# Self- and cross-attention pairs of a decoder: two program orders laid over each other, unit by unit

## The chip, the core and the metric

The kernel runs on one core of one Trainium2 chip. The metric is the device time of one execution in microseconds; the figure of a kernel is the median of its runs. One more execution was recorded by the hardware profiler, and the views shown below are of that execution. The engines are called by their short names: PE (TensorE), PEld (its weight loads), DVE (VectorE), ACT (ScalarE), POOL (GpSimd), SP (SyncE, which here issues nearly all DMAs).

## The reference

A decoder of twelve sub-layers with x of shape (4, 256, 128), each sub-layer `x = x + f(layernorm(x))`. Two stretches of it matter here, the pairs self-attention then cross-attention of layer 0 (sub-layers 0 and 1) and of layer 3 (sub-layers 9 and 10). Shortened:

```python
def attention(q, k, v, mask):             # 16 heads of width 8, B = 4 batches, 256 queries
    s = q @ k.T * 8 ** -0.5 + mask        # 256 keys (self) or 512 keys of the context (cross)
    return softmax(s) @ v                 # the softmax takes each row's maximum off
x = x + attention(heads(norm(x) @ Wq + bq), heads(norm(x) @ Wk + bk), ...) @ Wo + bo   # self
x = x + attention(heads(norm(x) @ Wq + bq), heads(ctx @ Wk + bk), ...) @ Wo + bo       # cross
```

The cross-attention's queries come from the x that the self-attention of the pair has made. Its keys and values come from the context, which is there from the start. Layer 0's cross-attention has a mask of one row for each batch, and layer 3's two attentions have full masks.

## The kernel before

An attention works in 16 steps (G = 16), one for each batch (4) and group of four heads (4). A step s has these parts, in a software pipeline: `a` are the scores for the maxima (PE, banks 0 to 3 of PSUM), reduced by DVE; `split` turns the maxima into three bf16 parts (POOL); `turn` transposes them (PE, bank 7), ACT copies them out, SP writes them into the rows of `qs` as further rows of the queries; `b` are the scores the other way round, with the maxima now taken off (PE, banks 4 and 5), and ACT's exponent; `av` multiplies by the values (PE, bank 6), `o` copies that out (ACT), `o_tp` transposes it (PE, bank 7) and DVE divides; after every fourth step `oT` and `y` transpose and multiply by the output weights (PE, bank 7) and DVE adds the result to x.

`order()` (L1118) yields these parts one after the other, and every engine walks through the same order and issues its own piece of each part. So the order on every queue is written by hand here, and a semaphore wait at the head of a queue holds everything behind it. `order_plain` (L1178) serves layer 0, `order_masked` (L1124) layer 3. The plain order runs over steps and, inside a step, units: four for the self-attention, eight for the cross-attention. The masked order runs over units alone, two to a step for self and four for cross. In both the last `a` part is followed by a tail in which only `b`, `av`, `o_tp`, `oT` and `y` of the last steps are left: units 68 to 91 of layer 0's self-attention, units 33 to 44 of layer 3's.

The two attentions of a pair know each other as `next` and `prev`. Keys of the cross-attention are made before the self-attention starts and split and spilled to DRAM beside it. The norm of x, and from it the cross-attention's queries, goes batch by batch: `stats_vector`, `h_vector`, `hT_tensor` and `q_tensor` (the names `n_stats`, `n_h`, `n_tp`, `nq` in the order) for batches 0 and 1 run inside the self-attention, those for batches 2 and 3 inside the cross-attention. The values (`val`, `v_sb`: four matmuls of 128x128 and a bias addition, for each of four chunks) are made in the cross-attention's first steps. `ahead_at` and `ahead_masked_at` (L511, L526) say at which step and unit; `ahead_sync` (L486) does the same for SP.

PE starts the cross-attention after it has waited for `x_done` of the self-attention, which DVE sets after the last addition to x (L2868, L2899). PE then waits in `stack_landed` (L764) for `first_quad`: the DMAs that bring the keys and queries of batch 0 and, for layer 0, the mask rows of all four batches.

The instructions of the rows below: L794 `a` scores, L872 and L860 their reductions (plain, and cross masked), L908 `turn`, L939 and L840 `b` scores, L803 masks added on PE, L1025 `av`, L1114 the addition to x, L563 values, L442 a subtraction of the query's parts, L264 POOL's addition of the output bias to x, L453 and L484 SP's spill and load of the cross queries.

## Time and profile before

| | us |
|---|---|
| median of 3 runs | 1468.37 |
| lowest, highest run | 1465.16, 1477.7 |
| span of the profiled execution | 1486.9 |
| its busy time on PE, DVE, ACT, POOL | 1203.9, 898.9, 707.4, 273.3 |
| mean granted clock of PE in it | 0.885 of full |

The profiled execution has no other time of its own than its span; that is 18.5 us, or 1.3%, above the median of the runs. The page cuts the span in 40 slices of 37.2 us. The first pair's self-attention lies in slices 1 to 3 and its cross-attention from there on (it starts at 110.8 us); the second pair's cross-attention starts at 1312.9 us, in slice 36. The granted clock is 1.00 at 2.4 GHz and 0.50 at 1.2 GHz; a value between them is a mean over both.

### The profile page before, as it was taken

The page shows a single profiled execution, that of the slowest core. Times are in us where ns is not written, and L with a number is a line of the kernel's source. Part 1 is how long each engine was busy: PE and PEld are TensorE (multiplying, and loading weights), DVE is VectorE, ACT ScalarE, POOL GpSimd, SP SyncE. Part 2 cuts the span into 40 slices and gives each one's busy share as a digit, 9 for nine tenths or more (in the row PEclk, how much of TensorE's full clock was granted, in tenths as well). Part 3 has the DMA queues.
Part 4 walks back from the last instruction along what each step waited for, and adds up shares of the span by engine and source line. Part 5 has one row for each costly group of instructions (what it writes and reads, how often), then busy time and mean ns, then how long its engine had stood idle before and what let it go on. Part 6 is the DMA issues. An engine that isn't in the chain of part 4 may idle for free. (4 is left out here: it accounts for less than half of the span.)

```text
span 1486.9 us, 26591 instructions
## 1 busy us (share of the span) xinstructions
PE 1203.9 (81%) x9482; PEld 745.1 (50%) x9489; DVE 898.9 (60%) x2315; ACT 707.4 (48%) x1440; POOL 273.3 (18%) x549
## 2 busy tenths in 40 slices
PE   4878997785786487567999999999957768979983
PEld 2333434683343487355666666666636733333331
DVE  5758865335667344775676676666741076667746
ACT  3654881221632121213665665666713425636663
POOL 3412111452010254100000000000006504211110
PEclk9897998897797699777999999999988878979996
DMA  7321242793401585000000000000046543211100
GB/s 189 89 57 44 67 140 100 230 290 116 115 30 64 169 252 181 28 1 1 1 1 1 1 1 1 1 1 1 1 112 193 169 131 82 54 42 50 48 6 15
DMA packets 87892, 114.34 MB, mean 77 GB/s; under 512 B 10945, under 2 KB 67982, under 8 KB 87294
## 3 DMA queue, kind: packets, MB, share of 16 engines
q1 hardware_dynamic: 83314, 103.52, 23.5%
q0 software_dynamic: 4448, 9.12, 2.0%
q8 instruction: 78, 1.28, 0.4%
q14 instruction: 52, 0.43, 0.1%
HBM read 85.79 MB, written 25.82 MB: 75 GB/s over the span
## 5 line engine op out<-in xcount | busy, mean ns | idle before, releaser
L1025 PE MATMUL ps<-probs,vaug 128*32 128x256 f32 (+1 forms) x1792 | 145.7, 399 | 15.3 <-ACT probs L991 8.5
L2508 DVE CUSTOM_DVE_ANT_0 wring<-ps,probs 128x768 f32<-128x768 f32 x128 | 122.6, 958 | 57.3 <-PE ps L2380 56.8
L2464 ACT COPY qs<-ps 128x768 f32<-128x768 f32 x128 | 102.3, 800 | 97.7 <-PE ps L2387 97.7
L982 ACT ACTIVATE probs<-ps 128x512 f32<-128x512 f32 x192 | 104.2, 595 | 63.7 <-PE ps L840 63.5
L872 DVE TENSOR_REDUCE mx<-ps 128x2 f32<-128x1024 f32 (+1 forms) x96 | 114.7, 1220 | 21.0 <-PE ps L794 20.7
L986 ACT ACTIVATE probs<-ps 128x512 f32<-128x512 f32 x192 | 106.4, 595 | 39.6 <-PE ps L939 37.6
L244 POOL TENSOR_TENSOR rstd<-veps,mhalf 128x8 f32<-128x8 f32 x12 | 19.9, 1660 | 569.5 <-DVE veps L229 539.9
L2446 ACT ACTIVATE wring<-wring,r 128x768 f32<-128x768 f32 x128 | 120.8, 944 | 2.9 <-DVE r L2511 2.9
L2387 PE MATMUL ps<-ident,wring 128*128 128x128 f32 x768 | 110.3, 281 | 3.2 <-DVE wring L2545 3.2
L2387 PEld LDWEIGHTS ps<-ident,wring 128*128 128x128 f32 x768 | 84.5, 141 | 39.4 <-issue 35.3
L1808 POOL DMA_INDIRECT scr_y<-probs x85 | 82.9, 975 | 99.4 <-DVE probs L1765 82.5
L2380 PE MATMUL ps<-probs 64*128 64x512 f32 (+1 forms) x512 | 99.9, 508 | 1.1 <-DVE r L2508 1.0
L860 DVE CUSTOM_DVE_ANT_0 wring<-ps,m3x 128x512 f32<-128x512 f32 x128 | 83.3, 689 | 26.1 <-PE ps L794 15.6
L794 PE MATMUL ps<-ks,qs 49*128 49x256 bf16 (+1 forms) x512 | 82.1, 362 | 12.5 <-DVE mx L872 3.5
L1557 PE MATMUL ps<-probs,wring 128*128 128x128 f32 x428 | 84.0, 304 | 8.9 <-DMA wring<-in_L_ffn_w 4.7
L2395 PE MATMUL ps<-qs,ks 128*64 128x256 f32 x768 | 89.9, 383 | 1.0 <-ACT qs L2464 1.0
L1758 DVE TENSOR_TENSOR probs<-gated,ps 128x256 f32<-128x256 f32 (+1 forms) x62 | 32.1, 519 | 88.1 <-ACT gated L1614 49.7
L2545 DVE TENSOR_SCALAR wring<-wring,r 128x768 f32<-128x768 f32 x128 | 79.5, 621 | 4.5
L1570 PE MATMUL ps<-wring,probs 128*128 128x128 f32 x428 | 64.1, 289 | 18.1 <-DVE probs L1758 8.5
L1557 PEld LDWEIGHTS ps<-probs,wring 128*128 128x128 f32 x428 | 67.9, 213 | 14.1 <-DMA wring<-in_L_ffn_w 7.5
L1614 ACT ACTIVATE gated<-ps 128x256 f32<-128x256 f32 (+1 forms) x62 | 28.6, 463 | 95.6 <-PE ps L1559 71.7
L1025 PEld LDWEIGHTS ps<-probs,vaug 128*32 128x32 f32 x1792 | 37.4, 110 | 65.8 <-issue 61.7
(346 smaller groups left out, 2387.0 us busy)
## 6 DMA issues: line engine op xcount, KB each, us to landing
wring<-in_L_ffn_w SPq DMA_DIRECT2D x19, 768.0 KB
wring<-in_L_ffn_w SPq DMA_DIRECT2D x32, 384.0 KB
wring<-in_L_ffn_w SPq DMA_DIRECT2D x19, 514.0 KB
qs<-scr_q SPq DMA_DIRECT2D x18, 192.0 KB
qs<-scr_qx SPq DMA_DIRECT2D x16, 192.0 KB
probs<-in_L_ffn_w SPq DMA_DIRECT2D x8, 384.0 KB
probs<-in_L_ffn_w SPq DMA_DIRECT2D x4, 768.0 KB
scr_k<-probs SPq DMA_DIRECT2D x21, 128.0 KB, 2.8
```

Source lines behind the costliest of these rows:

```text
L860: dve.tensor_tensor_reduce(wring[:, k % 2, r * S2:(r + 1) * S2], bank(self.banks(0, k)[r]), m3x[:, 0, a % 2 * S2:(a % 2 + 1) * S2], 1.0, - ...
L872: dve.tensor_reduce(out, src, AX.X, ALU.max, negate=True).then_inc(a_max.sem, 1)
L982: act.activation(probs[:, s % 2, 2 * c + r, kt0 * S:(kt0 + 2) * S], bank(self.banks(3, k)[r]), ACT.Exp).then_inc(p_exp.sem, 1)
L986: act.activation(probs[:, s % 2, 2 * c + r, kt0 * S:(kt0 + 2) * S], bank(4 + k % 2), ACT.Exp).then_inc(p_exp.sem, 1)
L1025: ins = pe.matmul(ps[32 * j:32 * j + 32, self.av_bank(s), q0:S], vaug[:, s % 2, kt, j, :], probs[:, s % 2, j, at:at + S - q0], start=(kt = ...
L1557: ins = pe.matmul(bank(k % 2)[:, at], gate[:, at], cols, start=True, stop=True)
L2380: ins = pe.matmul(bank(2 * j + lo // 512, 0, hi - lo), self.qT[rows, g % 2, k * P:(k + 1) * P], self.kT[rows, g % 3, lo:hi], start=True, s ...
L2387: ins = pe.transpose(self.buffer("turn", i, t * P, t * P + P), self.sc[:, i % 4, t * P:(t + 1) * P], ident[:, :])
L2395: ins = pe.matmul(self.buffer("sum", i, 0, S)[HW * j:HW * j + HW, :], self.v[:, i % 3, t, j * HW:(j + 1) * HW], self.pT[:, i % 2, j, t, :] ...
L2446: act.activation(self.sc[:, i % 4, :], self.sc[:, i % 4, :], ACT.Exp, bias=self.neg[:, i % 4:i % 4 + 1], accum_out=self.tot[:, i % 4:i % 4 ...
L2464: act.copy(self.pT[:, g % 2, j, :, k * P:(k + 1) * P], self.buffer("turn", i, 0, KV).rearrange("p (t n) -> p t n", n=P)).then_inc(self.out ...
L2508: dve.tensor_tensor_reduce(self.sc[:, s, :], src, self.maskb[:, u // (2 * PR), :], 1.0, -3.0e38, ALU.add, ALU.max, self.top[:, s:s + 1]).t ...
```

## The change

The separate orders are cut into functions of one unit (`plain_steps`, `causal_steps`, `masked_steps`), and `order()` of the self-attention now walks through both attentions of the pair. Up to the unit behind the self-attention's last `turn` it yields only the self-attention's parts. From there on each turn of the loop yields the self-attention's next unit and then the cross-attention's next unit, until the self-attention has none left. The cross-attention's own program and PE's wait for `x_done` are gone.

```diff
         def order(self):
-            return self.order_masked() if self.mask == "full" else ...
+            then = self.next
+            handoff = (33 if self.mask == "full" else 17 * self.u) if then else self.units()
+            for i in range(max(self.units(), handoff + then.units() if then else 0)):
+                if i < self.units():
+                    for step in self.steps(i):
+                        yield self, *step
+                if i >= handoff:
+                    for step in then.steps(i - handoff):
+                        yield then, *step
...
+        def partner_tensor(self, pe):
+            t = self.prev or self.next
+            if not t:
+                return
+            for sem, count in ((m_sb, t.turns), (o_div, t.outs), (oT_sb, t.turned_outs), (y_out, t.ys)):
+                if count and self.seen.get(sem.sem.name) != count:
+                    pe.wait_ge(sem.sem, sem.at(t.n, count))
+                    self.seen[sem.sem.name] = count
...
-            if s not in (0, 7, 11):
+            fused = s in subs and subs[s].prev
+            if s not in (0, 7, 11) and not fused:
                 pe.wait_ge(x_done.sem, x_done.at(s - 1, 1))
...
-    first_quad = counter("first_quad", [8 + 8 * int(c["mask"] == "row") if c["cross"] else 4 ...
+    first_quad = counter("first_quad", [8 + 2 * int(c["mask"] == "row") if c["cross"] else 4 ...
+    row_in = new("row_in")
...
+                if self.mask == "row" and s == NQ:
+                    pe.wait_ge(row_in, 32 * (B - 1))
...
-            if 12 <= g < 15:
-                self.q_spill_sync(sp, 0, g - 12)
-            if g == 15:
+            for k in ((0,), (1, 2))[g - 12] if g in (12, 13) else ():
+                self.q_spill_sync(sp, 0, k)
+            if g == 14:
                 self.q_load_sync(sp, 0)
...
-            if self.next and 7 <= o < 13 and o % 4 in (3, 0):
+            if self.next and o >= 7 and o % 4 in (3, 0):
                 yield ("n_tp" if o % 4 else "nq"), (o - 7) // 4, o
...
-                steps = {(0, 1): [("n_tp", 2), ("hT", 2)], (0, 3): [("nq", 2), ("qf", 2), ("n_h", 3)], (0, 6): [("val", 0)], (1, 0): [("val", 1)],
-                         (1, 1): [("v_sb", 0)], (1, 2): [("val", 2)], (1, 3): [("qr", 2), ("qp2", 2)], (1, 4): [("v_sb", 1)], (1, 5): [("v_sb", 2)],
-                         (2, 0): [("val", 3)], (2, 1): [("v_sb", 3), ("qp3", 2)], ...
+                steps = {(1, 0): [("val", 0)], (1, 2): [("val", 1), ("v_sb", 0)], (1, 4): [("nq", 2), ("qf", 2), ("v_sb", 1)],
+                         (1, 6): [("qr", 2), ("qp2", 2)], (1, 7): [("val", 2)], (2, 0): [("v_sb", 2), ("qp3", 2)], (2, 1): [("val", 3)],
+                         (2, 3): [("v_sb", 3)], (2, 4): [("n_h", 3)], ...
...
-                    if self.prev and s == 1:
-                        bias_gpsimd(pool, self.sub, self.norm, f"{self.name}_o")
+                if self.prev and s == 3:
+                    bias_gpsimd(pool, self.sub, self.norm, f"{self.name}_o")
```

Besides, PE gets waits that the barrier made needless before: the cross-attention's first use of each PSUM bank (in `a_tensor`, `b_tensor`, `masked_tensor`, `av_tensor`, `value_tensor`, `q_tensor`) waits for the self-attention's last reader of that bank, and `partner_tensor` does so for bank 7, which `turn`, `o_tp`, `oT` and `y` of both attentions share. POOL's addition of the output bias to x moves from the cross-attention's step 1 to step 3. `ahead_masked_at` moves the values by one or two units in the same way as `ahead_at`.

PE at the first hand-over. Before, from the self-attention's `oT` of batch 2 on (L939 is `b`, L1025 `av`, L1059 `o_tp`, L1104 `y`); the first `a` of the cross-attention stands seven rows below the last one shown:

```order
L1082 MATMUL ps<-ident,o 128x128 x2
L939 MATMUL ps<-qs,ks 128x256 x2
L1025 MATMUL ps<-probs,vaug 32x256 x4
L1059 MATMUL ps<-ident,osb 128x128 x2
L939 MATMUL ps<-qs,ks 128x256 x2
L1104 MATMUL ps<-w,oT 128x128 x2
L939 MATMUL ps<-qs,ks 128x256 x2
L1025 MATMUL ps<-probs,vaug 32x256 x4
L939 MATMUL ps<-qs,ks 128x256 x4
L1025 MATMUL ps<-probs,vaug 32x256 x4
L1059 MATMUL ps<-ident,osb 128x128 x2
L939 MATMUL ps<-qs,ks 128x256 x4
```

After, from the same place (L970 is `b`, L1058 `av`, L1093 `o_tp`, L1140 `y`, and L808 with `ks,qs 128x512` is `a` of the cross-attention):

```order
L1117 MATMUL ps<-ident,o 128x128 x2
L808 MATMUL ps<-ks,qs 128x512 x2
L970 MATMUL ps<-qs,ks 128x256 x2
L1058 MATMUL ps<-probs,vaug 32x256 x4
L1093 MATMUL ps<-ident,osb 128x128 x2
L970 MATMUL ps<-qs,ks 128x256 x2
L1140 MATMUL ps<-w,oT 128x128 x2
L808 MATMUL ps<-ks,qs 128x512 x2
L970 MATMUL ps<-qs,ks 128x256 x2
L1058 MATMUL ps<-probs,vaug 32x256 x4
L970 MATMUL ps<-qs,ks 128x256 x2
L808 MATMUL ps<-ks,qs 128x512 x2
```

The first `a` scores of the cross-attention, 18 rows behind this `oT` before, now stand right behind it and ahead of seven of the self-attention's last eight `b` parts; one more `a` follows every two units.

SP's queue at the same place. Before, from the maxima of step 13 on (`qs<-mT`; `scr_qx<-` are spills of the query's parts, `ks<-mrow` mask rows, `qs<-scr_qx` the load of batch 0's queries):

```order
L742 DMA qs<-mT 3x2x256 x2
L460 DMA ks<-mrow 1x8x512 x2
L453 DMA scr_qx<-lg 128x2x256
L742 DMA qs<-mT 3x2x256 x2
L460 DMA ks<-mrow 1x8x512 x2
L453 DMA scr_qx<-r 128x256
L742 DMA qs<-mT 3x2x256 x2
L484 DMA qs<-scr_qx 48x8x256 x2
```

After:

```order
L752 DMA qs<-mT 3x2x256 x2
L464 DMA ks<-mrow 1x8x512 x2
L457 DMA scr_qx<-lg 128x2x256
L457 DMA scr_qx<-r 128x256
L752 DMA qs<-mT 3x2x256 x2
L464 DMA ks<-mrow 1x8x512 x2
L489 DMA qs<-scr_qx 48x8x256 x2
L752 DMA qs<-mT 3x2x256 x2
```

The third spill and the load of the queries have moved ahead of one pair of `qs<-mT` each.

DVE at the second hand-over. Before, from the division of step 13 on (L1068 and L1069 are a division, L860 is the reduction of the cross-attention, in two rows):

```order
L1068 RECIPROCAL rsum<-ps 128x8
L1069 TENSOR_TENSOR o<-ps,rsum 128x2x32
L1068 RECIPROCAL rsum<-ps 128x8
L1069 TENSOR_TENSOR o<-ps,rsum 128x2x32
L1114 TENSOR_TENSOR x<-x,ps 128x256
L373 BN_STATS stats<-x 128x6 x2
L376 BN_AGGR mv<-stats 128x2 x2
L378 TENSOR_SCALAR veps<-mv 128x2
L2868 ISA
L860 ISA wring,mx<-ps,m3x 128x512
L860 ISA mx 128x1
L860 ISA wring,mx<-ps,m3x 128x512
```

After, from the self-attention's statistics of batch 2 on (L878 is the reduction, L390 the norm of batch 2, L1102 and L1103 a division):

```order
L380 TENSOR_SCALAR veps<-mv 128x2
L878 ISA wring,mx<-ps,m3x 128x512
L878 ISA mx 128x1
L878 ISA wring,mx<-ps,m3x 128x512
L878 ISA mx 128x1
L390 TENSOR_SCALAR h<-x,mv,rstd 128x128 x2
L878 ISA wring,mx<-ps,m3x 128x512
L878 ISA mx 128x1
L878 ISA wring,mx<-ps,m3x 128x512
L878 ISA mx 128x1
L1102 RECIPROCAL rsum<-ps 128x8
L1103 TENSOR_TENSOR o<-ps,rsum 128x2x32
```

Before, all of the self-attention's divisions and its last statistics stood ahead of the first reduction. Now two units of reductions (four instructions of L878 with a read each) stand ahead of the division of step 13.

## Rows read from the trace of the kernel before

**Rows 1.** Windows of the first pair; columns as its first line says.
```profile
core 0: us, PE busy (x) PEld busy (x) DVE busy (x) ACT busy (x) POOL busy (x), PEclk, DMA share, GB/s
93.78:139.10 45.32, 36.54 (x224) 15.48 (x226) 29.43 (x48) 18.71 (x41) 7.28 (x19) 0.70 0.16 41
...
97.30:104.00 6.70, 6.50 (x40) 2.24 (x40) 2.75 (x12) 3.80 (x8) 0.98 (x2) 0.51 0.49 117
104.00:111.00 7.00, 3.40 (x32) 1.56 (x28) 2.19 (x10) 1.21 (x4) 0.15 (x1) 0.98 0.01 2
111.00:119.00 8.00, 8.00 (x34) 4.71 (x33) 7.03 (x9) 1.25 (x3) 1.35 (x5) 0.57 0.01 3
119.00:126.00 7.00, 4.63 (x33) 2.75 (x33) 6.94 (x9) 2.11 (x5) 1.48 (x5) 0.91 0.21 58
126.00:138.50 12.50, 10.93 (x68) 3.16 (x66) 9.11 (x8) 6.90 (x14) 3.13 (x7) 0.51 0.12 32
150.00:200.00 50.00, 49.51 (x514) 20.64 (x516) 43.81 (x53) 43.62 (x87) 8.70 (x40) 1.00 0.22 58
```

**Rows 2.** The same view of the second pair.
```profile
1298.75:1343.21 44.46, 34.05 (x235) 14.96 (x233) 26.98 (x87) 15.56 (x35) 7.75 (x21) 0.73 0.15 37
1306.00:1313.00 7.00, 3.23 (x28) 1.54 (x28) 2.19 (x10) 1.36 (x4) 0.00 (x0) 0.97 0.04 11
1313.00:1322.60 9.60, 8.47 (x30) 4.81 (x30) 6.97 (x22) 1.25 (x3) 1.75 (x6) 0.50 0.01 2
1322.60:1329.60 7.00, 4.04 (x31) 2.22 (x31) 6.45 (x19) 1.75 (x4) 0.76 (x4) 0.99 0.21 57
1329.60:1343.00 13.40, 11.54 (x76) 3.85 (x76) 7.79 (x25) 5.20 (x12) 4.31 (x10) 0.50 0.12 32
1350.00:1430.00 80.00, 75.42 (x881) 28.07 (x873) 64.98 (x209) 56.82 (x120) 14.62 (x66) 1.00 0.16 40
```

**Rows 3.** Timeline of the first hand-over: start, us, engine, line, operation, idle before.
```profile
92.90 0.44 SPq L453 DMA_DIRECT2D scr_qx<-r  x1
...
93.78 0.38 PE L939 MATMUL ps<-qs,ks 52*128 52x256 bf16 x2
...
94.80 0.39 PE L939 MATMUL ps<-qs,ks 52*128 52x256 bf16 x2
...
95.96 0.93 SPq L484 DMA_DIRECT2D qs<-scr_qx  x2
...
110.79 0.39 PE L794 MATMUL ps<-ks,qs 49*128 49x512 bf16 x2 [1.54 <-DVEq L2868]
```

**Rows 4.** The second pair's first cross scores, the same view.
```profile
1312.94 0.61 PE L794 MATMUL ps<-ks,qs 49*128 49x512 bf16 x2 [1.54 <-DVEq L2868]
```

**Rows 5.** Timeline: `av` at half and full clock, a subtraction between them.
```profile
99.16 1.08 PE L1025 MATMUL ps<-probs,vaug 128*32 128x256 f32 x8
...
100.07 0.43 DVE L442 TENSOR_TENSOR gated<-gated 128x256 bf16<-128x256 f32 x1
...
104.57 0.64 PE L1025 MATMUL ps<-probs,vaug 128*32 128x256 f32 x8 [0.54 <-ACT osb L1042]
```

**Rows 6.** Bias addition, the subtraction beside it, and cross step 4's first scores.
```profile
125.32 2.35 POOL L264 TENSOR_TENSOR x<-x,brow 128x1024 f32<-128x1024 f32 x1
125.70 2.25 DVE L442 TENSOR_TENSOR r<-comb,lg 128x256 bf16<-128x256 f32 x1
...
139.10 0.39 PE L794 MATMUL ps<-ks,qs 49*128 49x512 bf16 x2
```

**Rows 7.** The second hand-over: third spill of the queries, and the unit behind 1298.75.
```profile
1295.60 0.42 SPq L453 DMA_DIRECT2D scr_qx<-r  x1
...
1301.33 0.40 PE L803 MATMUL ps<-m3a,identb 64*64 64x512 bf16 x2
```

**Rows 8.** DMA issues around the first hand-over: count, KB each, us to landing.
```profile
scr_qx<-gated SPq DMA_DIRECT2D x1, 192.0 KB, 3.4
```

**Rows 9.** The page, costliest groups: the plain reduction (count, busy, mean ns, idle before).
```profile
L872 DVE TENSOR_REDUCE mx<-ps 128x2 f32<-128x1024 f32 (+1 forms) x96 | 114.7, 1220 | 21.0 <-PE ps L794 20.7
```

More of the change, by code:

```diff
@@ L548, in evicted @@
         def evicted(self, o):
-            if self.next and 7 <= o < 13 and o % 4 in (3, 0):
+            if self.next and o >= 7 and o % 4 in (3, 0):
                 yield ("hT" if o % 4 else "qf"), (o - 7) // 4, o
@@ L1115, in y_vector, with units @@
                               ALU.add).then_inc(y_out.sem, 1)
-        def order(self):
-            return self.order_masked() if self.mask == "full" else self.order_causal() if self.mask == "causal" else self.order_plain()
-        def order_masked(self):
+        def units(self):
+            if self.mask == "full":
+                return G * self.u + self.behind + 4 * self.u
+            if self.mask == "causal":
+                return 2 * (G + 6)
+            return (G + self.lag + 4) * self.u
@@ new lines, in steps @@
+        def steps(self, i):
+            if self.mask == "full":
+                return self.masked_steps(i)
+            return (self.causal_steps if self.mask == "causal" else self.plain_steps)(*divmod(i, 2 if self.mask == "causal" else self.u))
+        def order(self):
+            then = self.next
[7 more added lines that the diff above has]
+                        yield then, *step
@@ L1178, in order_plain @@
-        def order_plain(self):
+            v = t - self.behind - n
+            o, d = v // n, v // n - 1
+            if t < G * n + self.behind:
+                yield "masked", t, 0
+            if v % n == 0 and 0 <= o < G:
+                yield from self.beside(o)
+            if self.cross:
+                if 0 <= o < G:
+                    yield "av", o, v % n
+                if v % n == 0 and last(d - 1):
+                    yield "y", (d - 1) // NQ, 0
+                if t % n == 1 and 0 <= t // n - 1 < G:
+                    yield "turn", t // n - 1, 0
+                if v % n == 2 and 0 <= d < G:
+                    yield "o_tp", d, 0
+                if v % n == 3 and last(d):
+                    yield "oT", d // NQ, 0
+            else:
+                if v % n == 1 and last(d):
+                    yield "oT", d // NQ, 0
+                if v % n == 0 and last(d - 1):
+                    yield "y", (d - 1) // NQ, 0
+                if 0 <= o < G:
+                    yield "av", o, v % n
+                if t % n == 0 and 0 <= t // n - 1 < G:
+                    yield "turn", t // n - 1, 0
+                if v % n == 0 and 0 <= d < G:
+                    yield "o_tp", d, 0
@@ new lines, in vector, with vector_step @@
+        def vector(self, dve):
+            for who, what, s, u in self.order():
+                who.vector_step(dve, what, s, u)
+        def vector_step(self, dve, what, s, u):
+            if what == "a":
+                self.a_vector(dve, s, u)
+            elif what == "masked" and s < G * self.u:
+                self.a_vector(dve, *divmod(s, self.u))
+            elif what == "b" and not self.maximum:
+                self.clip_vector(dve, s, u)
+            elif what == "o_tp":
+                self.div_vector(dve, s)
+            elif what == "y":
+                if self.n == 1 and s == B - 1:
+                    masks_vector(dve)
+                self.y_vector(dve, s)
+            elif what == "v_sb":
+                self.value_vector(dve, s)
+            elif what == "n_stats":
+                (self.next or self).stats_vector(dve, s)
+            elif what == "n_h":
+                (self.next or self).h_vector(dve, s)
+            elif what == "qr":
+                (self.next or self).q_r_vector(dve, s)
+            elif what == "qp3":
+                (self.next or self).q_p3_vector(dve, s)
@@ new lines, in scalar, with scalar_step @@
+        def scalar(self, act):
+            for who, what, s, u in self.order():
+                who.scalar_step(act, what, s, u)
+        def scalar_step(self, act, what, s, u):
+            if what == "b":
+                self.b_scalar(act, s, u)
+            elif what == "masked" and s >= self.behind:
+                self.b_scalar(act, *divmod(s - self.behind, self.u))
+            elif what == "o":
+                self.o_scalar(act, s)
+            elif what == "oT":
+                self.oT_scalar(act, s)
+            elif what == "turn":
+                self.turn_scalar(act, s)
+                if self.next and s < B:
+                    self.next.key_p2_scalar(act, s)
+            elif what == "hT":
+                if u >= 0:
+                    act.wait_ge(av_mm.sem, av_mm.at(self.n, u + 1))
+                (self.next or self).hT_scalar(act, s)
+            elif what == "qf":
+                if u >= 0:
+                    act.wait_ge(av_mm.sem, av_mm.at(self.n, u + 1))
+                (self.next or self).q_scalar(act, s)
+            elif what == "qp2":
+                (self.next or self).q_p2_scalar(act, s)
```

289 lines of the change are left out of this document (121 added, 168 removed).

## The prediction

> **What bounds the kernel now.** The table of busy times has PE at 1203.9 of 1486.9 us, far ahead of DVE, so work of other engines beside a busy PE is mostly hidden. I cut each pair into windows. In the middle of the first pair's cross-attention PE is busy 49.51 of 50 us and DVE 43.81, at full clock; in the second pair's PE is busy 75.42 of 80 us and DVE 64.98 [rows 1, 2]. That is what a well filled stretch looks like, and there is nothing to gain there. Around the hand-overs it differs. From 93.78 us, when the self-attention has made its last turn of maxima, to 139.10 us, when the cross-attention's step 4 begins, 45.32 us pass, with PE busy 36.54 us at a mean clock of 0.70 and DVE 29.43 [rows 1]. The second pair has the like from 1298.75 to 1343.21 us: 44.46 us, PE 34.05 at 0.73, DVE 26.98 [rows 2]. I then asked what PE waits for. The timeline puts the idle time before the first cross scores at 110.79 and at 1312.94 us down to DVEq L2868, the barrier after the last addition to x [rows 3, 4]. Before each barrier there are 7 us in which PE is busy only 3.40 and 3.23 us, because the tail of the self-attention is a chain of round trips; behind it, in the first cross steps, DVE is the busy one (7.03 of 8.00 us) [rows 1, 2]. So two stretches with complementary needs lie one behind the other.
>
> The windows show a second cost. After each thin stretch PE's granted clock is near 0.5, that is 1.2 GHz: at 97.3 to 104, 111 to 119 and 126 to 138.5 us in the first pair, at 1313 to 1322.6 and 1329.6 to 1343 us in the second [rows 1, 2]. The same `av` group takes 1.08 us there and 0.64 us at full clock [rows 5], a factor of 0.6. Of PE's 36.54 us, 25.43 lie in the three half-clock windows (6.50 + 8.00 + 10.93); at full clock they would be 15.3, so PE's work in the first stretch is 26.4 us. In the second, 20.01 us lie in such windows (8.47 + 11.54) and become 12.0, which makes 26.0 us.
>
> **The change part by part.** *Removed:* the wait for `x_done`, and with it the serial order of tail and start. *Added:* nothing that computes. Every matmul, reduction and DMA is issued as before, so only their overlap counts. *The sum for the first pair*, to the same point (cross step 4's first scores, [rows 6]): DVE needs 29.4 us. Of this 1.8 us is one subtraction (L442) that took 2.25 us beside POOL's bias addition of 2.35 us [rows 6] and would take 0.43 as elsewhere [rows 5], since the bias addition now runs two steps later, where DVE has reductions only. That leaves 27.6. A filled stretch takes 50 / 43.81 = 1.14 times its DVE work [rows 1], hence 31.5. DVE can't begin at once: I add 2.0 us until its first cross reduction (below), and 2.0 us for the first half-clock spell. This one I expect to stay, because what comes before it (up to 97.3 us) is not merged; PE's 6.5 us of it hold only 3.9 of work, a loss of 2.6 of which DVE's slack covers a part. Together 35.5 us against 45.3, **9.8 us less**. Bounds of this term: if PE and DVE overlapped without loss, the longer of the two would be about 30 (PE 26.4 + 2.6 + the stall of 1.4; DVE 27.6 + 2.0), 15 us less; with nothing overlapped, 0.
>
> *The second pair:* DVE 27.0 us times 80 / 64.98 = 1.23 is 33.2, and 1.5 us until the first reduction gives 34.7 against 44.5, **9.8 us less**. PE's 26.0 us fit with room. I take no half-clock spell here, since the clock is still 0.97 from 1306 to 1313 us, at the end of the tail [rows 2].
>
> *The load of the queries.* PE's first cross scores wait for it, and the self-attention's `b` parts are queued behind them, then ACT's exponents and `av`. In the second pair the third spill left at 1295.60 us, behind the maxima of step 14 [rows 7], and the load followed the maxima of step 15; now both move up by one, the load to about 1295.6. With 3.4 us to landing, the time of a spill of the same 192 KB [rows 8], it is there at 1299, before PE is through the unit whose successor began at 1301.33 [rows 7]. Hidden. In the first pair the load moves from 95.96 to about 93.1 us: it takes the place of the spill at 92.90, a few tenths later because the spill now stands ahead of the maxima [rows 3]. PE reaches the new scores at about 94.8, where the next `b` stood [rows 3]. The load lands between 96.2, if it is as fast as 3.1 us, and 97, at 3.4 us behind its second half's issue: a stall of 1.4 to 2.2 us; I take 1.4 because nothing else is on the queues then. It is inside the 2.0 us above.
>
> *The moved values, queries and mask rows.* All are the same instructions, inside the sum. The mask rows of batches 1 to 3 no longer hold the start; only the two for batch 0 do, and those are old by then. The row of batch 1 waits for the self-attention's last `b`, and the maxima of cross step 0 are queued behind it on SP. That `b` comes near 106 us by my order, the maxima at about 113: hidden, and worth at most 1.4 us (one pair of issues) if not.
>
> *The added waits.* DVE's divisions and additions to x, four and two in each tail, now stand behind cross reductions, and PE's `o_tp`, `y` and `turn` wait for them. The wait costs nothing while PE has cross work queued ahead of it, and a reduction, 1.2 us [rows 9], each where it has not. The factors 1.14 and 1.23 come from stretches with just this coupling.
>
> The sum is 9.8 + 9.8 = 19.6 us. What follows each pair starts from its end and moves up whole. The profiled span of 1486.9 would be 1467.3; against the median of 1468.4, 18.5 us lower, the same 19.6 us give **1449 us**.
>
> Of the subtraction: the Trainium skill, SBUF — State Buffer, "Who interferes with whom", says a DVE instruction with two SBUF inputs is held while GpSimd reads SBUF, and one with at most one is not. By that rule the trace's 2.25 us [rows 6] is such a hold and the reductions, which read PSUM, run freely beside the bias addition. Were they held too, the 1.8 us would stay where they are and the time would be 1451.
>
> **The rivals.** *The clock stays low.* PE and DVE now wait for each other in short turns all through the merged stretch, and the clock might fall again there as it did at 126 and 1329.6 us. For it: those falls came after 7 us with PE busy 4.63 and 4.04 [rows 1, 2], and the merged stretch isn't far from that. Against it: a merged stretch has PE busy 26.4 of 35 us or more, 75%, and in the filled stretch the same coupling holds 1.00. Price: a spell of 12.5 us, as at 126, in each pair loses 0.4 x 12.5 = 5 us each: 1459 us. The skill's TensorE: Matmul & The Clock Gate, "A second HAM failure mode: psum-queue depth-cycling", tells of a clock that swings because of just such small pauses; the windows of the filled stretches show none.
>
> *Nothing overlaps.* Each unit's self part and cross part wait for one another, so that the merged units take as long as both did: 1467 us. Against it speaks that the first `a` and `b` parts use different banks and no data of each other. For it, that all queues keep their order.
>
> *Slower.* The place is the six waits of PE for DVE in each tail (four divisions, two additions). If each is exposed for a reduction of 1.2 us or two, and nothing overlaps besides, 12 x 1.2 to 1.5 = 16 us come on top: 1484. It decides once exposed waits exceed the overlap, some 1.6 us for each of the 12.
>
> *More than forecast.* PE and DVE overlap without loss: 15 + 14 us, 1439.
>
> **How the numbers follow.** The forecast with its own range 1441 to 1456 has 0.62, the low clock 0.20, nothing overlapped 0.10, slower 0.04, more than forecast 0.04. The range 1440 to 1463 leaves out nothing overlapped, slower and part of the last, some 0.18. A measurement of this kernel tells about 1% from no change, that is 14.7 us: faster means under 1453.7. The forecast gives that in nine of ten cases (0.57), more than forecast 0.04, a low clock in one of the pairs only 0.04: 0.65. Slower is 0.04, and the rest 0.31.
>
> **What would show it.** The same two stretches, from the first `b` after the last turn to cross step 4 in the first pair and to unit 14 in the second, take 35.5 and 34.7 us. The wait for DVEq before the first cross scores is gone. PE waits 1.4 us for the load of the queries near 94.8. The clock is low once after 97 us and not again in the pair, and near 1.00 in the second pair. DVE is over 80% busy between the hand-over and step 4. The 2.25 us subtraction takes 0.43. The prediction is wrong if the clock falls again inside the merged stretch, if DVE is under 75% busy there with PE idle before `o_tp` or `y`, or if a wait for `first_quad` exceeds 3 us.

## The result, and the profile after

| | before | after |
|---|---|---|
| median, us | 1470.97 (4 runs, 1465.16 to 1477.7) | 1450.86 (4 runs, 1449.63 to 1456.17) |
| ratio after to before | | 0.9873, 95% interval 0.9838 to 0.9907 |
| span of the profiled execution | 1486.9 | 1447.8 |
| mean granted clock of PE in it | 0.885 | 0.894 |

The changed kernel is 1.27% faster by the ratio of the runs, some 18.7 us on 1471; the medians are 20.1 us apart. The two profiled spans differ by 39.1 us, but not all of that is the change. From the fourth cross turn of pair 1 to turn 15 of pair 2 the program is the same in both kernels (but for the end of POOL's bias addition in its first microsecond), and this part took 1156.04 us before (142.51 to 1298.55) and 1137.89 after (134.02 to 1271.91). A second execution of the changed kernel, in an experiment below, took 1153.57 us for it. So some 18 us of the 39 are differences between executions. I read the two stretches of the prediction alone.

Line numbers move: L808 is `a`, L890 and L878 its reductions (plain, masked), L937 `turn`, L970 `b`, L817 masks on PE, L571 values, L660 their bias addition on DVE, L446 the query's subtraction, L265 the output bias on POOL, L464 mask rows, L489 the load of the cross queries, L752 the maxima into `qs`. In a window's row the number behind x counts the instructions, and the value third from the end is the mean granted clock.

Windows of the changed kernel, pair 1, from the first `b` after the self-attention's last turn (91.70 us) to cross step 4's first scores (130.76); this answers to [rows 1]:

```profile
core 0: us, PE busy (x) PEld busy (x) DVE busy (x) ACT busy (x) POOL busy (x), PEclk, DMA share, GB/s
91.70:130.76 39.06, 31.35 (x224) 14.10 (x224) 27.49 (x48) 18.31 (x42) 4.83 (x18) 0.78 0.16 44
95.90:105.30 9.40, 9.28 (x51) 3.51 (x53) 6.32 (x16) 3.54 (x7) 0.93 (x2) 0.50 0.09 24
105.30:111.00 5.70, 5.64 (x56) 3.28 (x51) 4.46 (x7) 1.35 (x3) 0.80 (x4) 0.99 0.02 3
...
114.00:117.00 3.00, 1.41 (x13) 0.67 (x11) 3.00 (x5) 1.66 (x4) 0.83 (x4) 1.00 0.38 108
...
120.00:122.50 2.50, 1.19 (x10) 0.37 (x8) 2.50 (x3) 2.07 (x6) 0.58 (x2) 0.99 0.00 1
122.50:129.50 7.00, 6.60 (x46) 2.11 (x48) 5.62 (x7) 3.70 (x8) 1.49 (x6) 0.52 0.20 57
```

The stretch took 39.06 us, where 45.32 were before and 35.5 were forecast: 6.3 us less instead of 9.8. The clock is at 0.50 for 9.4 us right from the first cross scores, and again at 0.52 for 7 us from 122.5 on. Ahead of this second fall PE is busy 1.41 of 3 us (114 to 117) and 1.19 of 2.5 us (120 to 122.5) while DVE is busy all the time; between the two PE is well filled, 2.83 of 3 us.

The same view of pair 2, from 1272.11 us to the turn at 1304.39; it answers to [rows 2]:

```profile
1272.11:1304.39 32.28, 27.45 (x234) 12.86 (x233) 25.64 (x85) 14.83 (x34) 5.38 (x20) 0.89 0.15 39
1275.00:1290.00 15.00, 13.47 (x122) 6.84 (x120) 13.83 (x50) 6.13 (x15) 1.98 (x7) 1.00 0.17 46
...
1292.50:1304.39 11.89, 9.85 (x74) 4.34 (x75) 8.79 (x26) 4.92 (x10) 2.32 (x8) 0.71 0.14 36
1293.00:1297.00 4.00, 3.94 (x22) 2.39 (x24) 3.29 (x11) 1.32 (x3) 0.20 (x1) 0.57 0.00 1
1297.00:1300.00 3.00, 1.53 (x20) 0.57 (x16) 2.79 (x8) 2.01 (x4) 0.29 (x1) 1.00 0.46 116
1300.00:1304.39 4.39, 4.39 (x38) 1.38 (x35) 2.21 (x7) 1.59 (x4) 1.34 (x6) 0.61 0.06 17
```

Here 32.28 us stand against 44.46 before and 34.7 forecast: 12.2 us less. From 1275 to 1290 us both engines are full, PE 90% and DVE 92% busy at full clock. Only behind that, from 1292.5 on, the mean is 0.71: two short low spells of the clock, with 1.00 between them.

Timeline of the first hand-over (SPq is SP's DMA queue; behind "x" the idle time before and its releaser), answering to [rows 3]:

```profile
91.01 0.65 SPq L464 DMA_DIRECT2D ks<-mrow  x1
...
91.70 0.38 PE L970 MATMUL ps<-qs,ks 52*128 52x256 bf16 x2
91.70 0.95 SPq L489 DMA_DIRECT2D qs<-scr_qx  x2
...
95.90 0.61 PE L808 MATMUL ps<-ks,qs 49*128 49x512 bf16 x2 [3.12 <-DMA qs<-scr_qx]
...
96.62 1.23 DVE L890 TENSOR_REDUCE mx<-ps 128x2 f32<-128x1024 f32 x1 [3.09 <-PE ps L808]
```

The wait for DVEq is gone, and PE now reaches the cross scores at 92.78 (95.90 less 3.12) and waits 3.12 us for the load of the queries. The load was issued from 91.70 on, behind a mask row, and released PE 4.2 us later. In three more profiled executions of this pair's program (they belong to the experiments below) the wait was 2.94, 3.70 and 3.85 us. DVE's first cross reduction starts at 96.62, 4.9 us into the stretch.

Timeline of the second hand-over, which answers to [rows 4, 7]:

```profile
1268.96 0.93 SPq L489 DMA_DIRECT2D qs<-scr_qx  x2
...
1274.69 0.39 PE L808 MATMUL ps<-ks,qs 49*128 49x512 bf16 x2
```

The load leaves 5.7 us ahead of the scores, and PE doesn't wait. Timeline of DVE, POOL and PE near 117 and 132 us, answering to [rows 6]:

```profile
116.78 0.41 DVE L446 TENSOR_TENSOR r<-comb,lg 128x256 bf16<-128x256 f32 x1
...
116.92 1.16 PE L571 MATMUL ps<-w,ctxT 128*128 128x128 f32 x8 [1.32 <-DVE v L660]
...
132.42 2.37 POOL L265 TENSOR_TENSOR x<-x,brow 128x1024 f32<-128x1024 f32 x1
133.46 2.43 DVE L890 TENSOR_REDUCE mx<-ps 128x2 f32<-128x1024 f32 x2 [0.96 <-PE ps L808]
```

The subtraction takes 0.41 us where it took 2.25. The bias addition now runs beside two reductions, which take 2.43 us together, as long as elsewhere (1.22 and 1.23 each).

### The profile page after: what moved, and what is told of

It reads as the page before. It is cut to its first block, busy times and chain, and to the rows that moved or that the text cites. A ratio compares the mean times of both kernels' runs of the same rounds, so it can differ in the third digit from the quotient of the medians.

```text
span 1447.8 us, 26607 instructions
## 1 busy us (share of the span) xinstructions
PE 1185.1 (82%) x9482; PEld 735.6 (51%) x9489; DVE 896.5 (62%) x2315; ACT 708.3 (49%) x1440; POOL 273.0 (19%) x549
## 4 chain that ended last, share of the span: by engine, by line
PE 62%; DVE 14%; DMA 6%; ACT 6%; issue 5%; POOL 4%; SPq 3%; DVEq 0%; another core or an unknown queue 0%; ACTq 0%; POOLq 0%
PE ps L2447 7%; PE ps L2454 6%; PE ps L1058 6%; PE ps L2462 6%; PE ps L808 4%; PE ps L2434 3%; PE ps L817 3%; PE ps L1624 2%; PE ps L970 2%; PE ps L2428 2%; DMA wring<-in_L_ffn_w 2%; PE ps L1637 2%; PE ps L2961 2%; PE ps L1626 2%; PE ps L1093 2%
## 5 line engine op out<-in xcount | busy, mean ns | idle before, releaser
L1058 PE MATMUL ps<-probs,vaug 128*32 128x256 f32 (+1 forms) x1792 | 145.2, 398 | 12.1 <-ACT probs L1022 7.1
L890 DVE TENSOR_REDUCE mx<-ps 128x2 f32<-128x1024 f32 (+1 forms) x96 | 115.0, 1221 | 21.3 <-PE ps L808 20.7
L878 DVE CUSTOM_DVE_ANT_0 wring<-ps,m3x 128x512 f32<-128x512 f32 x128 | 83.2, 688 | 20.0 <-PE ps L808 11.7
L808 PE MATMUL ps<-ks,qs 49*128 49x256 bf16 (+1 forms) x512 | 80.6, 354 | 9.9 <-DMA qs<-scr_qx 3.1
L1624 PE MATMUL ps<-probs,wring 128*128 128x128 f32 x428 | 80.3, 294 | 7.9 <-DMA wring<-in_L_ffn_w 5.6
L1058 PEld LDWEIGHTS ps<-probs,vaug 128*32 128x32 f32 x1792 | 37.3, 110 | 61.3 <-issue 56.6
L2447 PEld LDWEIGHTS ps<-probs 64*128 64x128 f32 x512 | 44.3, 186 | 47.0 <-issue 38.0
```

The source lines that it names most:

```text
L808: ins = pe.matmul(bank(at[r], i * self.keys, (i + 1) * self.keys), self.qv(s, c, r, ROWS_A, t * P, (t + 1) * P), self.kv(s, c, r, ROWS_A), ...
L890: dve.tensor_reduce(out, src, AX.X, ALU.max, negate=True).then_inc(a_max.sem, 1)
L1058: ins = pe.matmul(ps[32 * j:32 * j + 32, self.av_bank(s), q0:S], vaug[:, s % 2, kt, j, :], probs[:, s % 2, j, at:at + S - q0], start=(kt = ...
L1624: ins = pe.matmul(bank(k % 2)[:, at], gate[:, at], cols, start=True, stop=True)
L2447: ins = pe.matmul(bank(2 * j + lo // 512, 0, hi - lo), self.qT[rows, g % 2, k * P:(k + 1) * P], self.kT[rows, g % 3, lo:hi], start=True, s ...
```

## The experiments

All stretches below run from turn 15 (the self-attention's last) to the cross-attention's fourth turn, since these marks are in every kernel. The work in them is nearly the same everywhere: 29.2 to 29.9 us of DVE in pair 1 (31.7 before), 30.8 to 31.6 in pair 2. Each median stands beside that of the kernel before on the same chip; there the kernel before takes 1486.82 to 1487.58 us, not 1470.97. The last two columns are one profiled execution's stretches, in us, and the mean clock in them:

| kernel | median, us | ratio to before (95%) | pair 1 | pair 2 |
|---|---|---|---|---|
| before | 1470.97 | 1 | 49.11 at 0.72 | 51.75 at 0.77 |
| changed | 1450.86 | 0.9873 (0.9838, 0.9907) | 42.71 at 0.80 | 39.64 at 0.91 |
| serial | 1482.84 | 0.9965 (0.9938, 0.9991) | 47.78 at 0.75 | 45.72 at 0.89 |
| first pair only | 1473.79 | 0.9904 (0.9867, 0.9942) | 41.96 at 0.80 | 47.64 at 0.82 |
| second pair only | 1473.64 | 0.9926 (0.989, 0.9962) | 45.74 at 0.85 | 38.64 at 0.96 |
| masks behind | 1469.20 | 0.9878 (0.9843, 0.9912) | 41.52 at 0.79 | 41.98 at 0.84 |
| changed, again | 1466.81 | 0.9892 (0.9844, 0.9939) | 43.03 at 0.80 | 38.55 at 0.96 |
| filled | 1464.60 | 0.9847 (0.9806, 0.9889) | 40.67 at 0.87 | 39.63 at 0.91 |
| masks behind and filled | 1466.22 | 0.9872 (0.9826, 0.9919) | 37.04 at 0.95 | 38.63 at 0.96 |
| one step later | 1467.51 | 0.9898 (0.9854, 0.9941) | 39.05 at 0.91 | 38.61 at 0.96 |
| changed, third | 1468.69 | 0.9887 (0.9854, 0.992) | 43.12 at 0.80 | 40.05 at 0.91 |
| masks behind and filled, again | 1466.90 | 0.9886 (0.9851, 0.9921) | 36.28 at 0.95 | 38.63 at 0.96 |
| one step later, again | 1468.81 | 0.9885 (0.9851, 0.9919) | 43.20 at 0.72 | 38.62 at 0.96 |
| serial, bias at step 1 | 1485.39 | 0.9992 (0.9964, 1.0019) | 51.91 at 0.67 | 49.40 at 0.79 |

The pair 2 column shows how much one execution may differ from the next: ten rows have the changed kernel's program there. Six of them took 38.55 to 38.64 us at 0.96, three 39.63 to 40.05 at 0.91, and one 41.98 at 0.84. So a difference of up to 3 us between two single stretches proves nothing by itself.

**Serial: everything of the change but the merge.**

```diff
-            handoff = (33 if self.mask == "full" else 17 * self.u) if then else self.units()
+            handoff = self.units()
```

> The changed kernel with the hand-over put back to the end of the self-attention in both pairs: its new order functions, added waits, earlier query load and later values stay, only the overlap is gone. If the overlap is the whole of the gain (the prediction's sum), this is the kernel before within 0 to 3 us less, because PE no longer waits for the barrier's semaphore (1.54 us idle in each pair before): ratio to before 0.998 to 1.000. If the new placement of the values and of the query load brings part of it by itself, the ratio is near 0.995 or below. If the added waits cost something that the overlap hides, it is above 1.002.

The rest of the change (values one or two units later, bias at step 3, the queues' new order, no `x_done`) brings 0.35% by itself, 4.0 us between the medians. The merge is what is left, about 0.8% (0.9873 to 0.9892 for the changed kernel against 0.9965). Windows of the serial kernel's two stretches:

```profile
93.01:140.79 47.78, 38.15 (x260) 16.53 (x256) 29.68 (x50) 21.56 (x48) 7.39 (x23) 0.75 0.18 46
1298.21:1343.93 45.72, 35.00 (x310) 15.90 (x311) 31.58 (x101) 20.12 (x45) 7.92 (x26) 0.89 0.14 40
```

In pair 2 this is 6.0 us less than before at the same DVE work (31.62 before), and PE's busy time falls from 41.01 to 35.00 us for 311 and 310 matmuls in the record: the mean clock is 0.89 instead of 0.77. After PE's first thin spot in the cross steps the clock fell before (1329.6 us on, [rows 2]) and did not here. That the moved values did this isn't shown: it is one execution of each kernel.

**One pair alone.** The first-pair-only kernel has `self.units()` in place of 33, the second-pair-only kernel in place of `17 * self.u`.

> Only the first pair (layer 0) is merged, the second pair runs one attention after the other. The prediction's sum gives 9.8 us for this pair: ratio 0.9933. The trace of the changed kernel, read over the same stretch, gives 45.3 - 39.1 = 6.3 us: ratio 0.9957. The rival that the pairs share the gain evenly and one profile is off would show 0.9935 here and in the other half.

> Only the second pair (layer 3) is merged. The prediction's sum gives 9.8 us: ratio 0.9933. The trace of the changed kernel gives 44.5 - 32.3 = 12.2 us: ratio 0.9917. If the parts add up, the two halves' gains together are the 18.7 us of the whole change.

```profile
92.64:134.60 41.96, 34.15 (x260) 15.38 (x256) 29.59 (x50) 21.06 (x48) 7.27 (x23) 0.80 0.20 52
```

```profile
1293.45:1332.09 38.64, 33.03 (x310) 14.52 (x311) 30.79 (x101) 19.97 (x45) 7.97 (x26) 0.96 0.17 47
```

The first row is of the first-pair-only kernel, the second of the other. Against the serial kernel pair 1 gains 5.8 us in its stretch and pair 2 7.1 us; by the medians each merge is worth 9.1 and 9.2 us, each with an uncertainty of some 6 us. Neither merge needs the other: each merged stretch is as short alone as in the changed kernel. That the medians add up holds only within these uncertainties (18.3 us for the two alone, some 0.8% or 12 us for both). The pair that is not merged has the serial kernel's program once more, and is as long as there within 2.1 us, both ways: 45.74 us at 0.85 in pair 1 and 47.64 at 0.82 in pair 2. Against the kernel before, the rest of the change thus brings 4.1 or 6.0 us in pair 2 by the execution taken.

**Masks behind: the queries' load ahead of the last mask rows on SP.**

```diff
-            if self.mask == "row" and g in (10, 13, 14):
-                self.mask_sync(sp, (0, 2, 3)[(10, 13, 14).index(g)])
+            if self.mask == "row" and g == 10:
+                self.mask_sync(sp, 0)
...
+            if self.mask == "row" and g in (13, 14):
+                self.mask_sync(sp, g - 11)
```

> The changed kernel with one edit on SP's queue: the mask rows of batches 2 and 3 are issued behind the third spill and behind the load of batch 0's queries instead of ahead of them (1.4 us of issue each). In the changed kernel PE is idle for 3.12 us before its first cross scores, for this load. Theory that the load is late because of what SP issues ahead of it: the load leaves 1.4 us earlier, the idle time falls to about 1.7 us, and the time by 1 to 1.5 us against the changed kernel (ratio to before about 0.9865). Rival, that the landing of the two halves of 192 KB sets it or that the clock's low spell swallows it: the idle time stays over 2.5 us or the time doesn't move.

```profile
90.75 0.93 SPq L489 DMA_DIRECT2D qs<-scr_qx  x2
91.72 1.43 SPq L464 DMA_DIRECT2D ks<-mrow  x2
...
94.66 0.61 PE L810 MATMUL ps<-ks,qs 49*128 49x512 bf16 x2 [1.73 <-DMA qs<-scr_qx]
```

The wait falls from 3.12 to 1.73 us, 1.4 us, which is one pair of mask issues (1.43), and the stretch by 1.2 us (by 0.4 against the first-pair-only kernel, whose pair 1 is the changed one's). So the mask rows ahead of the load are some 1.4 us of the stall; the prediction had left them where they were. The clock did not gain by it: it was low behind the shorter wait too, 0.79 over the stretch. The ratio is that of the changed kernel within its interval.

**Filled: does PE's pause cost the clock?**

```diff
+            if k == 0 and n == 1:
+                pe.wait_ge(a_max.sem, a_max.at(0, a_max.totals[0] - 1))
+                for _ in range(2):
+                    pe.matmul(bank(0), wt(f"{self.name}_q"), ctxT[:, 0:512], start=True, stop=True, ...)
             if a == 0:
                 self.stack_landed(pe, s)
```

> The changed kernel once more, beside the next three on one chip. Both theories: 1.2 to 1.3% faster than the kernel before (ratio 0.987), with PE waiting about 3 us for the queries' load before the cross-attention's first scores in pair 1, and low clock from there for some 9 us and again near 122 us.

> Two more matmuls, 128x512 in f32 out of data that is there, are put on PE ahead of its wait for the first quad of the cross-attention in pair 1; their result is overwritten. They fill about 1.7 of the 3.1 us that PE waits there. Theory A (the pause makes the clock fall, and the low clock stretches PE's work behind it): the granted clock stays at 1.00 from 96 to 104 us, the stretch from turn 15 to the fourth cross turn shrinks from 42.7 by 1 to 3 us, and the kernel runs 1 to 2.5 us faster than the changed one. Theory B (the clock costs little there, since DVE's reductions are the bound of these units): the clock may rise but the stretch stays at 42.7 within 0.7 us, and so does the time.

> Masks of batches 2 and 3 behind the queries' load on SP's queue, as in the run with the masks behind, which left PE a wait of 1.73 us, and one more 128x512 matmul (0.85 us) in this wait. Theory A (clock): 1.00 from 95 to 104 us, 2.5 to 4 us faster than the changed kernel over both edits. Theory B (no gain from the clock): as the masks alone, 1.2 us less in the stretch than the changed kernel.

The changed kernel repeats itself closely, 43.03 us at 0.80, with a wait of 3.70 us for the load. In the filled kernel 1.86 us of the wait remain and the stretch is 2.4 us shorter. In the third, whose wait is filled but for 0.67 us, it is 6.0 us shorter. The first cross scores of the three, in this order:

```profile
98.50 0.61 PE L808 MATMUL ps<-ks,qs 49*128 49x512 bf16 x2 [3.70 <-DMA qs<-scr_qx]
98.41 0.39 PE L812 MATMUL ps<-ks,qs 49*128 49x512 bf16 x2 [1.86 <-DMA qs<-scr_qx]
97.40 0.39 PE L814 MATMUL ps<-ks,qs 49*128 49x512 bf16 x2 [0.67 <-DMA qs<-scr_qx]
```

Windows of the same three:

```profile
93.33:136.36 43.03, 34.46 (x261) 15.37 (x256) 29.68 (x50) 21.07 (x48) 7.28 (x23) 0.80 0.20 51
```

```profile
93.36:134.03 40.67, 34.62 (x264) 15.87 (x260) 29.30 (x50) 21.20 (x48) 7.32 (x23) 0.87 0.21 54
```

```profile
94.40:131.44 37.04, 30.41 (x262) 14.38 (x258) 29.40 (x50) 21.02 (x48) 7.29 (x23) 0.95 0.22 59
...
96.00:99.00 3.00, 2.33 (x18) 0.68 (x16) 1.53 (x2) 1.80 (x5) 0.00 (x0) 1.00 0.29 75
99.00:102.00 3.00, 2.62 (x28) 1.27 (x27) 2.00 (x10) 1.99 (x5) 0.06 (x1) 1.00 0.18 50
```

DVE's work is the same in all three within 0.4 us, and PE's instructions within three; what changes is the clock. In the third it is 1.00 up to 120 us, the whole first low spell is gone, and PE's busy time falls by 4 us though it has a matmul more. That speaks for theory A in the stretch, and against B. Not all of the 6 us is the clock's: against the kernel with the masks behind alone (41.52 us, no filler), where the scores start about as early (3.2 us behind turn 15 against 3.0), 4.5 us are left. In the time of the whole kernel it is less clear: the medians lie 2.2 and 0.6 us below the changed kernel's, hence the next runs.

**One step later: no load to wait for.**

```diff
-            handoff = (33 if self.mask == "full" else 17 * self.u) if then else self.units()
+            handoff = (33 if self.mask == "full" else 18 * self.u) if then else self.units()
```

> Hand-over of pair 1 one step (four units) later: the cross-attention's first scores stand behind the self-attention's turn 15 and four more units. Theory A (the load's wait and the clock's fall cost more than the overlap of four units): PE waits under 0.5 us for the load, no low clock at 96 us, and the time is 1 to 2 us below the changed kernel's. Theory B (the overlap itself is what counts; each unit pair overlapped saves about 9 us / 24 = 0.4 us): 1.5 us slower than the changed kernel in pair 1.

```profile
93.18:132.23 39.05, 31.77 (x260) 14.69 (x256) 29.19 (x50) 21.35 (x48) 7.37 (x23) 0.91 0.22 56
```

PE has no wait for the load, and the stretch is 39.05 us at 0.91. The four units of overlap that were given up are not missed in it. But the median is 0.7 us above the changed kernel's, which fits neither theory's time.

**The last two and the yardstick again, and the serial kernel's 4 us.**

> The changed kernel as the yardstick for the next two. Both theories: 43 us from turn 15 to the fourth cross turn in pair 1, and a ratio of 0.987 to 0.989.

> The kernel with the masks behind and one filler matmul again, since its stretch was 6 us shorter than the changed kernel's while its median was only 0.6 us lower. Theory A (the stretch's gain is one of the whole kernel, the medians of five runs were too few): stretch 37 us, median 3 to 6 us below the changed kernel's. Theory C (it is given back later, or was of that one profiled execution): the stretch is 39 us or more, or the median is within 1.5 us of the changed kernel's.

> The hand-over of pair 1 one step later again, for the same reason: its stretch was 4 us shorter than the changed kernel's and its median 0.7 us higher. Theory A: stretch 39 us, median 2 to 4 us below the changed kernel's. Theory C: the stretch is 41 us or more, or the median is within 1.5 us of the changed kernel's.

Windows of masks behind and filled, then of one step later, each the second execution:

```profile
93.30:129.58 36.28, 30.47 (x263) 14.47 (x258) 29.40 (x50) 21.00 (x48) 7.30 (x23) 0.95 0.21 57
```

```profile
92.03:135.23 43.20, 37.21 (x260) 16.45 (x256) 29.57 (x50) 21.47 (x48) 7.40 (x23) 0.72 0.20 51
```

The filled wait repeats: 36.28 us at 0.95, against 43.12 at 0.80 for the changed kernel beside it. The later hand-over does not: the same kernel took 39.05 us at 0.91 once and 43.20 at 0.72 the other time, where PE ran at half clock at 96 us already. So the gain of that edit was of one execution (theory C).

This leaves a rival to what the filler seemed to show, that the clock falls or stays here whatever PE's wait is. Take the 6 us that begin 4 us behind turn 15. In these rows the first is of the serial kernel and the second of the second-pair-only kernel, which has the same program up to there; neither has a wait for the load:

```profile
97.01:103.01 6.00, 5.23 (x40) 1.85 (x40) 2.70 (x11) 3.97 (x9) 0.98 (x2) 0.72 0.20 58
96.88:102.88 6.00, 5.06 (x51) 2.17 (x52) 2.61 (x11) 4.10 (x9) 0.98 (x2) 1.00 0.25 68
```

Of the six executions without a wait for the load the clock fell in four (means of 0.50 to 0.72: the kernel before, both serial kernels, and the later hand-over's second) and held 1.00 in two (second pair only, and the later hand-over's first). With an unfilled wait of 1.73 to 3.85 us it fell in all five (0.50 or 0.51). With one filler and at most 0.67 us of wait it held 1.00 in both. So the fall does not need the wait, and two executions are too few to say that the filler prevents it: without any wait, two of six held as well. The wait is likely to make the fall surer; more isn't shown.

For the whole kernel the eleven runs of each give means of 1468.7 us (changed), 1465.8 (masks behind and filled) and 1468.1 (one step later), with standard errors of 1.1 to 1.3. The filled wait with the masks behind is thus worth 2.9 us, give or take 3.3: neither that it is worth nothing nor that it is worth the 6 us of the two profiled stretches is settled.

Last, the bias addition back at the cross-attention's step 1, in the serial kernel:

```diff
-                if self.prev and s == 3:
+                if self.prev and s == 1:
```

> The serial kernel (hand-over only after the self-attention's last unit) with POOL's bias addition back at the cross-attention's step 1; all else as in the serial run, which was 4.0 us faster than the kernel before. Theory D (these 4 us come from the bias addition that no longer meets the query's subtraction): the subtraction takes over 2 us again and the gain falls to under 1.5 us. Rival: they come from the values, of which the matmuls are placed a step later, and from waits and clock there; then the subtraction alone brings back 1.8 us on DVE at most and the gain stays at 2.5 us or more.

Most of the 4 us seem gone (ratio 0.9992, its interval overlaps the serial kernel's), but neither theory had it right. D was not put to the test: the subtraction took 0.42 us again, since the bias addition did not come beside it, so what the collision of the two is worth in time stays open. (DVE's work in pair 1 is 29.68 and 29.86 us in the two serial kernels, 31.66 before, so the 1.8 us came back in neither.) The addition was held up:

```profile
130.84 2.35 POOL L265 TENSOR_TENSOR x<-x,brow 128x1024 f32<-128x1024 f32 x1 [7.43 <-DVE h L390]
...
133.61 0.19 POOL L905 CAST mpart<-mx 128x8 bf16<-128x8 f32 x1
```

The addition to x must wait until the norm of batch 3 has read x, and the change has moved this norm (`n_h` 3) later. At step 1 POOL's queue stands for 7.43 us, and the split of the maxima behind it starts at 133.61. That is 3.00 us behind the start of the two reductions at 130.61; in the serial kernel it is 1.38 us (131.25 behind 129.87), so the hold cost 1.6 us there. Turns 2 and 3 come later (136.43 and 143.71 against 134.81 and 140.79), at a clock of 0.67 over the stretch instead of 0.75. The move of the bias belongs to the move of the norm: the norm's move alone seems to lose most of what both bring. How much of the 4 us is the order and how much the clock that goes with it stays open.

## Why the prediction was right, and where its terms were off

The time was 1449 us forecast, 1450.86 measured; the gain 19.6 and 18.7 us. In the traces both stretches together gained 6.3 + 12.2 = 18.5 us. The total is right and the split, 9.8 and 9.8, is not: pair 1 gained 3.5 us less than forecast and pair 2 gained 2.4 more, so the closeness of the total is in good part luck. The mechanism holds, the overlap of tail and start: the serial kernel, which lacks nothing else of the change, gains 0.35% instead of 1.1 to 1.3%. Of the prediction's three signs of being wrong two came: the clock fell again inside the merged stretch of pair 1, and the wait for `first_quad` exceeded 3 us (3.12). Step by step:

*DVE's work.* 27.6 us forecast in pair 1, 27.49 measured; the 1.8 us of the subtraction came back as taken (0.41 us). In pair 2 it was 25.64 instead of 27.0; one masked reduction with its read, 0.77 us of it, starts behind the turn now (27 instead of 28 in the record come ahead of it).

*The start, 2.0 and 1.5 us.* This term was too small: the first cross reduction came 4.9 us into the stretch in pair 1 and, at 1276.43, 4.3 us in pair 2. In pair 2 that cost little, since DVE had the tail's addition, division and statistics to do from 1274.80 on. In pair 1 the load was the reason: 3.12 us instead of 1.4. PE came to the scores where the prediction had it, 1.1 us into the stretch. But the load's issue began with the stretch, not 0.7 us ahead of it, and PE was released 4.2 us after this first issue, where the prediction's 1.4 us took 3.1 and its upper end, 2.2 us, took 3.9. (In the two repeats of the changed kernel it was 4.7 and 5.0 us.) For 3.1 us the prediction shows no row, and 3.4 was a spill's landing, which was a poor stand-in for the load's. The run with the masks behind gives 1.4 us back. This start is where most of pair 1's shortfall lies: 2.9 of the 3.5 us.

*The factors 1.14 and 1.23.* From the first cross reduction on, pair 1 took 34.1 us (to 130.76) for the 27.1 us of DVE work that were left, 1.26 times it; pair 2, from 1274.80 on, 29.6 us for 25.2, which is 1.17. For pair 1 the forecast had 33.5 us for this part, 31.5 and the low spell's 2.0, so it was off by 0.6 only; but the factor of 1.14 alone was too small. With the clock at 0.95 the longer stretch of the experiments is 37.04 us for 29.40 of DVE, or 1.26, start included; at 0.80 it is 1.45.

*The low clock.* One spell in pair 1 and none in pair 2 were forecast. Pair 1 had two, 9.4 and 7.0 us long, pair 2 two short ones (0.57 over 4 us and 0.61 over 4.4). The prediction named the second fall as what would prove it wrong, and priced that rival at 5 us for each pair. It did come in both. In pair 1 the two spells together with the longer wait cost about what the rival said: the same work took 42.7 to 43.1 us at 0.80, 41.5 at 0.79 with the wait cut by moving the masks, and 36.3 to 37.0 at 0.95, so 6 us in all and some 5 for the clock. In pair 2 the ten executions of one program lie between 38.55 us at 0.96 and 41.98 at 0.84. I had argued that a merged stretch keeps PE 75% busy on average; but the spots of 1.41 of 3 us and 1.19 of 2.5 us ahead of the fall show that the average says little. The Trainium skill, TensorE: Matmul & The Clock Gate, "A second HAM failure mode: psum-queue depth-cycling", tells of a clock that swings between its two levels when PE pauses often between groups of matmuls. This trace agrees as far as the swing goes: 0.50, then 0.99, then 0.52 in pair 1, where the filled stretches of before hold 1.00. Which pauses bring it about isn't shown.

*What made up for it.* Pair 2 gained 2.4 us more than forecast. Between 1275 and 1290 us DVE is 92% busy, against the 81% of the stretch that gave the factor. And by the executions with a serial pair 2, a third to a half of pair 2's gain isn't overlap: 4.1 and 6.0 us of it come with the rest of the change, at a higher clock. Both are counted from a single execution of the kernel before. At equal clock the merge itself is worth about 6 us in pair 2 (45.72 at 0.89 against 39.64 and 40.05 at 0.91). In pair 1 it is about 4 (serial 47.78 at 0.75 and, in the second-pair-only kernel, 45.74 at 0.85; merged 43 at 0.80).

*DVE's share.* Over 80% was forecast, 70% (27.49 of 39.06) and 79% (25.64 of 32.28) were measured. Pair 1 is under the prediction's mark of 75%, but the mark wanted PE idle before `o_tp` or `y` as well; the idle time was at the load.

*What was right besides.* The wait for `x_done` is gone in both. The second pair's load is hidden. The added waits of PE for divisions and additions to x cost next to nothing in pair 1: PE's groups of instructions there (busy, mean ns, idle before) show 0.0 us of idle time ahead of `o_tp` (L1093) and 0.1 ahead of `y` (L1140):

```profile
L1093 PE MATMUL ps<-ident,osb 128*128 128x128 f32 x8 | 2.2, 368 | 0.0
L1140 PE MATMUL ps<-w,oT 128*128 128x128 f32 x8 | 1.8, 365 | 0.1
```

The reductions run freely beside POOL's bias addition (1.22 us each), as the Trainium skill, SBUF — State Buffer, "Who interferes with whom", has it for a DVE instruction with at most one input in SBUF.

## What to carry to other kernels

Where the end of one part and the start of the next wait on different engines, laying one order over the other works even if every queue keeps its order; here it was worth 4 to 6 us of about 45 at each place, at equal clock. Then look at the first instruction of the second part: its inputs are now due earlier, and what is left ahead of them on the DMA queue is paid in the wait (1.4 us here for one pair of issues). Don't take PE's mean busy share for an argument that the clock holds: this stretch had 80%, and the clock was low twice in it. And don't settle an effect of the clock by one trace of each kernel: one and the same program took 39.05 us and 43.20 us for its stretch. And if a step is moved, look for the one on another queue that must move with it, as POOL's bias addition had to with the norm.

## What the runs showed of the hardware

Two things I had not expected. First, what goes with a filled pause: one more matmul of 128x512 f32 (1.02 us by the trace) in PE's wait, with the wait at 0.67 us or less, went with a clock of 1.00 through the 9 us in which it had been low, in both executions recorded, and with stretches of 37.04 and 36.28 us. With 1.73 us of wait left, or 1.86 behind two matmuls, the clock fell all the same, in the second case later and for less long (0.81 and 0.62 in the windows from 99 to 105 us instead of 0.50). That the filler is the cause is likely, not shown, since the clock held in two of six executions without a wait too.

Second, the clock isn't a matter of the program alone: the later hand-over, with nothing changed and the same idle times ahead of it from turn 15 on, ran once at 0.91 and once at 0.72 over the same stretch, 4.2 us apart. The serial program did the like in pair 1 (47.78 us at 0.75 and 45.74 at 0.85). The Trainium skill, TensorE: Matmul & The Clock Gate, "Part 1: The HAM clock gate", calls the clock's rise at the start of a kernel variable from run to run in one and the same kernel; these rows show the like for its fall in the middle of one. What decides between the two here stays open.
